# Local attention on one core: where two copies of turned q and k stand in ScalarE's and VectorE's order

## The reference, cut to what matters

```
q, k, v = split(shift_tokens(x) @ Wqkv)
q = l2norm(q) * q_scale; k = l2norm(k) * k_scale
q, k = rotary(q), rotary(k)                       # per token tables
out = softmax(8 * q k^T, own and previous window) @ v
x = x + out @ Wo
x = x + (a * gelu(gate)) @ W2 + b2                # a, gate = split(layernorm(shift_tokens(x)) @ W1 + b1)
```

## Time and profile before

| what | value |
|---|---|
| median of 3 runs | 6108.04 us (6103.54 to 6109.04) |
| the profiled execution | 6121.37 us, its span 6119.5 us |
| mean granted TensorE clock | 0.942 of full speed |
| PE busy | 5367.4 us (88%) |
| DVE busy | 4246.4 us (69%) |
| ACT busy | 3928.5 us (64%) |
| POOL busy | 2706.7 us (44%) |

### The profile page before, as it was taken

The page is one execution under the profiler, slowest core; times in us unless marked ns, Lnnn a source line. Parts: engine busy times, 40 slices in busy tenths (PEclk is TensorE's granted clock), DMA queues, the critical chain, the costliest instruction groups (busy, mean ns, idle before and its releaser), DMA issues. The chain is left out here.

```text
span 6119.5 us, 121575 instructions
## 1 busy us (share of the span) xinstructions
PE 5367.4 (88%) x41154; PEld 3816.5 (62%) x41154; DVE 4246.4 (69%) x16112; ACT 3928.5 (64%) x11510; POOL 2706.7 (44%) x2578
## 2 busy tenths in 40 slices
PE   7885699999999999997489999999999999697989
PEld 5674366666666666665256666666666666464678
DVE  4453788788787887885378878888788788454522
ACT  2211588888888888884168888888888888222333
POOL 0000556556566565562065655656556556130000
PEclk9996899999999999998589999999999999697999
DMA  0000000000000000000000000000000000000000
GB/s 11 22 1 2 22 1 12 9 12 9 1 15 6 12 9 12 8 1 4 21 1 5 12 6 12 9 12 9 1 15 6 12 8 1 5 2 4 2 29 8
DMA packets 30964, 53.45 MB, mean 9 GB/s; under 512 B 7688, under 2 KB 17168, under 8 KB 29712
## 3 DMA queue, kind: packets, MB, share of 16 engines
q1 hardware_dynamic: 30352, 45.66, 2.4%
HBM read 44.60 MB, written 1.05 MB: 7 GB/s over the span
## 5 line engine op out<-in xcount | busy, mean ns | idle before, releaser
L1784 PE MATMUL bank<-wA,next_rowT 128*128 128x512 f32 x2304 | 1197.1, 631 | 268.8 <-DVE kT L2113 68.2
L1983 ACT ACTIVATE pairs<-pairs,negmax 128x128 f32<-128x128 f32 (+1 forms) x3072 | 1241.2, 421 | 18.9 <-DVE negmax L2088 15.5
L1960 POOL TENSOR_TENSOR turnA<-raw,ropes 128x512 f32<-128x512 f32 x768 | 970.0, 1272 | 262.4 <-ACT raw L2007 229.8
L2088 DVE CUSTOM_DVE_ANT_0 pairs<-bank,bands,big 128x128 f32<-128x128 f32 (+1 forms) x3072 | 942.2, 363 | 80.4 <-PE bank L1716 73.5
L1967 POOL TENSOR_TENSOR qk<-turnA,turnB 128x512 f32<-128x512 f32 x768 | 976.6, 1272 | 0.0
L1944 POOL COPY spread<-recip 128x256 f32<-128x256 f32 x768 | 305.2, 397 | 1220.9 <-DVE recip L2097 1216.3
L1784 PEld LDWEIGHTS bank<-wA,next_rowT 128*128 128x128 f32 x2304 | 379.3, 191 | 696.2 <-issue 353.2
L1990 ACT ACTIVATE pairsT<-bank 128x512 f32<-128x512 f32 x768 | 469.7, 612 | 266.2 <-PE bank L1729 265.8
L1983 ACT ACTIVATION_READ_ACCUMULATOR pairs<-pairs,negmax 128x1 f32 x3072 | 634.5, 207 | 0.0
L285 POOL TENSOR_TENSOR rstd<-vareps,neg_half 128x2 f32<-128x2 f32 x56 | 39.0, 696 | 1293.3 <-DVE vareps L256 891.4
L2127 DVE TENSOR_TENSOR turnB<-bank,ropes 128x512 f32<-128x512 f32 x768 | 522.6, 680 | 0.2 <-issue 0.2
(11 more groups left out here) (306 smaller groups left out, 11358.7 us busy)
## 6 DMA issues: line engine op xcount, KB each, us to landing
wA<-in_wt_wqkv SPq DMA_DIRECT2D x72, 256.0 KB, 2.8
wB<-in_wt_wo SPq DMA_DIRECT2D x12, 512.0 KB, 3.4
wC<-in_wt_w SPq DMA_DIRECT2D x12, 341.0 KB, 2.9
wD<-in_wt_w SPq DMA_DIRECT2D x12, 192.0 KB, 2.3
big<-in_e_up SPq DMA_DIRECT2D x1, 2048.0 KB
big<-in_e_down SPq DMA_DIRECT2D x1, 2048.0 KB
scl<-in_wt_scales SPq DMA_DIRECT2D x12, 128.0 KB, 3.3
X<-in_x SPq DMA_DIRECT2D x8, 128.0 KB, 2.5
```

Of the source, the lines that this page charges most:

```text
L1784: pe.matmul(side_bank(i)[:, :], c.next_rowT[:, t * P:(t + 1) * P], wqkv[:, k * 512:(k + 1) * 512], start=True, stop=True).then_inc(s.chunk ...
L1960: g.tensor_tensor(c.turnA[:, m % 2, :].rearrange("p (h d) -> p h d", h=8), c.raw[:, m % 4, :].rearrange("p (h d) -> p h d", h=8), cos, ALU ...
L1983: last = a.activation(tile, tile, ACT.Exp, scale=-1.0, bias=c.negmax[:, 2 * p + side, t:t + 1], accum_out=c.pair_sums[:, p % 4, t, side:si ...
L2088: last = v.tensor_tensor_reduce(c.pairs[:, 2 * (p % 4) + side, AT[t]:AT[t] + SPAN[t]], c.bank[side][:, AT[t]:AT[t] + SPAN[t]], c.bands[:, ...
```

## The change

In slot 0 ScalarE's copy of the turned q moves from between the two sides of the exponentials to ahead of both; in slot 3 it stays where it was. In slot 3 VectorE's copy of the turned k moves from behind the maxima to ahead of them; in slot 0 it stays behind. No instruction is added or taken out, and nothing changes on TensorE, GpSimd or the DMA queue.

```diff
@@ act_window
+                if p == 0:
+                    act_copy_q(a, T, COPY_LATE_QKT_SLOTS[p])
                 for side in range(2):
                     if p + 1 < PAIRS:
                         act_probs(a, T, p + 1, side)
                     elif following:
                         act_probs(a, T + 1, 0, side)
-                    if side == 0 and p in COPY_LATE_QKT_SLOTS:
+                    if side == 0 and p == 3:
                         act_copy_q(a, T, COPY_LATE_QKT_SLOTS[p])
@@ dve_window
+                if p == 3:
+                    dve_copy_k(v, T, COPY_LATE_QKT_SLOTS[p])
                 if p + 2 < PAIRS:
                     dve_negmax(v, T, p + 2)
                 elif following:
                     dve_negmax(v, T + 1, p + 2 - PAIRS)
-                if p in COPY_LATE_QKT_SLOTS:
+                if p == 0:
                     dve_copy_k(v, T, COPY_LATE_QKT_SLOTS[p])
```

## The result

The changed kernel takes 6059.64 us (median of 4 runs, 6058.55 to 6063.89) against 6107.84 us for the kernel before (median of 4 runs): a ratio of 0.9921, 95% interval 0.9909 to 0.9934, 48.2 us less. The prediction said 6066 us. The profiled execution took 6063.89 us, its span 6062.1, which is 57.4 us less than the profiled span of before. The profiled execution of before, 6121.37 us, is none of these four.

The account below looks back on a forecast made before the run. VectorE, unbroken from slot 2 to the end of slot 5, was taken as the bound. Slot 0's 0.45 us and slot 3's 0, over 94 turns, gave 42 us off 6108.04: 6066 us, range 6042 to 6100.

Parts of the forecast that it names:

- TensorE's stalls stand beside VectorE's chain; only slot 0's counts: Slots 0 and 3: of TensorE's waits for q and k, only slot 0's 0.88 us lie on the turn's loop.
- q is there at 40.83, the exponentials end 0.26 us later, VectorE regains it and starts its stretch 0.45 us earlier: Slots 0 to 2: copying q earlier delays the exponentials 0.26 us, yet VectorE starts its slot 2 stretch 0.45 us earlier.
- VectorE runs without a break to the end of slot 5: Slots 2 to 5: VectorE, busy 19.37 of 20.08 us, works unbroken and sets when chunk 11 can start.
- Slot 3 brings 0: Slot 3: copying k earlier gains 0, bounds 0 and 1.15 us, since TensorE then waits for rotations in slots 4 and 5.
- 94 x 0.45 = 42 us: Whole kernel: 0.45 us saved in each of 94 turns, 47 per transformer, makes 42 us.
- The forecast turn of 44.5 us: One turn, from one addition to Y to the next, was to take 44.5 us instead of 44.98.
- Both stalls counting: Slots 0 and 3: TensorE keeps 0.63 + 1.15 = 1.78 us a turn, 167 us, giving 5941 us; chance 0.06.
- Nothing moves: Slots 0 to 2: ScalarE's 0.26 us delay reaches VectorE's stretch; under 0.13 us a turn left, 6096 to 6120 us; chance 0.14.
- the slower rival: Slots 0 and 1: ScalarE's wait for q passes to VectorE's reciprocal, costing 24 us, giving 6132 us; chance 0.06.

Follow-up runs that it names:

- slot 3 alone: Kernel before with only VectorE's copy of k moved ahead of the maxima in slot 3; 6088.65 us, ratio 0.9960.
- slot 0 alone: Kernel before with only ScalarE's copy of q moved ahead of the exponentials in slot 0; 6079.72 us, ratio 0.9949.

## Why the prediction was right, step by step

- *TensorE's stalls stand beside VectorE's chain; only slot 0's counts.* Shown in the ordinary turn, by the two halves of the change: 0.34 us and 0.00.
- *q is there at 40.83, the exponentials end 0.26 us later, VectorE regains it and starts its stretch 0.45 us earlier.* Right: ScalarE waits 0.40 us, the reciprocal came 0.25 us later, the stretch starts 0.44 earlier. Chunk 0 starts 0.54 us earlier, not 0.63; slot 0's wait is 0.34, not slot 3's 0.25. Slot 3's wait for k, forecast at 0.5 to 0.8, is 0.39: the prediction's own terms give 1.35 + 0.63 - 1.60 = 0.38.
- *VectorE runs without a break to the end of slot 5.* This step failed. GpSimd's addition holds one instruction in slot 2, so VectorE's 0.44 us went into a longer hold; what arrived was 0.34 us, by way of GpSimd. That the two are so close is luck. With the hold gone the edit is worth 0.43. The long instruction stood in the trace of before at 1.18 us, as busy time: rows 5 counts 19.37 of 20.08 us busy, and about 1 us of that was VectorE being held. Without it VectorE's share is no larger than TensorE's 18.43, so the comparison of busy times did not show VectorE as the bound; TensorE's waits for rotations do.
- *Slot 3 brings 0.* Right for the chain, wrong for the kernel: about 25 us through the clock. The reading that failed is that several turns with the same waits stand for all. They had the same waits, but 20 of 86 were 1.3 us longer. The prediction had no term for the clock.
- *94 x 0.45 = 42 us.* Measured 48.2: 32 from the chain, and the rest, about 16 in these runs, from the clock. The forecast turn of 44.5 us was 44.64. The two errors have opposite signs, so the sum came out closer than its terms: that 6066 lies within 7 us of 6059.64 is in part luck.
- *The rivals.* Both stalls counting, 167 us, is refuted by slot 3 alone, which took out 1.15 us of wait a turn and left the turn as it was. The Trainium skill (Perfetto Trace Analysis, Optimization Strategies), which the prediction read as counting both stalls in full, speaks of the engines "that are blocking the critical path"; here the wait for k was not on it. *Nothing moves* is refuted by slot 0 alone: 0.34 us a turn, not under 0.13. For the slower rival the reciprocal would have had to come 0.62 us later; it came 0.25 later.

## What to carry to other kernels

A wait of the busiest engine is worth its length only if nothing else arrives just behind it: follow each stall to the next place where the engine would wait, and test the halves of an edit apart. Before one turn is read for all, list the lengths of all turns; a second length shows a cost that waits don't. And an instruction that takes many times what its size asks for is a wait in disguise, however busy its engine looks: see what the neighbour does until it ends.

## What the runs showed of the hardware

- Idle time of 1.35 us on TensorE in an otherwise busy turn was followed, in 20 of 86 turns, by a fall of the granted clock (a mean of 0.58 over 4 us in the turn shown), worth 1.3 us a turn. Ten useless transposes in the gap took this away, and so did spreading the same idle time over shorter waits. Why the clock falls in some of these turns and not in others (20 of 86 behind 1.35 us, 12 of 86 behind 1.55 us, in one execution each) was not settled.
- VectorE's scalar operation of two numbers a partition, 0.17 us alone, took 1.24 us while GpSimd added two 128x512 tiles, until 0.03 us after GpSimd was done; in 90 turns each of the kernels before and after such an instruction ended 0.02 to 0.05 us behind that addition. Moving that addition by one slot took 0.99 us off each turn.
